# A one-core graph network layer: another order of the work within a step on TensorE, ScalarE and VectorE

## What is computed

```python
h = jnp.maximum(_layernorm(x, axis=-1), 0.0)
msg_input = jnp.concatenate([h[src], h[dst]], axis=1)
for t in range(4):
    m = jax.nn.relu(msg_input @ W1[t] + b1[t]) @ W2[t] + b2[t]
    msgs = msgs + jnp.where((edge_type == t)[:, None], m, 0)
agg = jax.ops.segment_sum(msgs, dst, num_segments=num_nodes)
gi = agg @ W_ih.T + b_ih          # i_r, i_z, i_n
gh = h @ W_hh.T + b_hh            # h_r, h_z, h_n
r = jax.nn.sigmoid(i_r + h_r)
z = jax.nn.sigmoid(i_z + h_z)
n = jnp.tanh(i_n + r * h_n)
out = x + (1.0 - z) * n + z * h
```

## Time and profile before

| | us |
|---|---|
| median of 3 runs | 1842.27 |
| lowest, highest | 1839.33, 1843.18 |
| profiled execution, its own time | 1840.2 |
| its span in the trace | 1838.3 |
| TensorE busy in the span | 1667.1 |
| VectorE, ScalarE, GpSimd busy | 1595.2, 1494.6, 1178.9 |

### The profile page before, as it was taken

The page is one execution under the profiler, slowest core; times in us unless marked ns, Lnnn a source line. Parts: engine busy times, 40 slices in busy tenths (PEclk is TensorE's granted clock), DMA queues, the critical chain, the costliest instruction groups (busy, mean ns, idle before and its releaser), DMA issues.

```text
span 1838.3 us, 43100 instructions
## 1 busy us (share of the span) xinstructions
PE 1667.1 (91%) x10182; PEld 1416.6 (77%) x10182; DVE 1595.2 (87%) x4186; ACT 1494.6 (81%) x3401; POOL 1178.9 (64%) x1982
## 2 busy tenths in 40 slices
PE   0226799999999999999999999999999999999998
PEld 0125688888888888888888888888888888888787
DVE  8597798989888988898889888989899989898776
ACT  0025789889888898898888888889898889888795
POOL 5777777776776777777765656666666566666310
PEclk9999899999999999999999999999999999999999
DMA  2225677777777776777677777777777777777653
GB/s 70 51 48 139 168 195 194 192 192 192 198 187 193 191 194 186 187 192 191 187 193 187 190 188 187 187 190 189 189 190 188 190 186 192 189 187 191 161 136 100
DMA packets 477071, 319.72 MB, mean 174 GB/s; under 512 B 106705, under 2 KB 463009, under 8 KB 476962
## 3 DMA queue, kind: packets, MB, share of 16 engines
q10 hardware_dynamic: 261792, 156.12, 28.6%
q1 hardware_dynamic: 185730, 106.99, 25.3%
q0 software_dynamic: 29440, 55.47, 11.8%
HBM read 211.65 MB, written 106.72 MB: 173 GB/s over the span
## 4 chain that ended last, share of the span: by engine, by line
PE 73%; ACT 8%; issue 4%; ACTq 3%; DVE 2%; DMA 0%; SPq 0%; POOL 0%; DVEq 0%; POOLq 0%
PE bank L1329 16%; PE bank L1331 12%; PE bank L1330 12%; PE bank L1409 10%; PE bank L1399 5%; PE bank L1391 5%; PE bank L1421 3%; PE bank L1420 3%; PE bank L1437 3%; ACT n_h L1194 3%; PE bank L1447 3%; ACT n_zc L1282 2%; ACTq L1211 2%; ACT e_r L1270 2%; ACTq L1232 2%
## 5 line engine op out<-in xcount | busy, mean ns | idle before, releaser
L580 POOL DMA_INDIRECT e_x<-in_x,rows_now x816 | 799.6, 980 | 241.7 <-issue 233.4
L1177 ACT ACTIVATE e_h<-e_x,shift,rstd 128x128 f32<-128x128 f32 x816 | 355.3, 493 | 93.6 <-DVE shift L1048 93.6
L1194 ACT ACTIVATE n_h<-n_x,shift,rstd 128x128 f32<-128x128 f32 x784 | 362.8, 489 | 2.1 <-issue 2.1
L1329 PE MATMUL bank<-n_h_hi,whh_hi 128*128 128x512 f32 x588 | 263.0, 447 | 25.3 <-ACT n_zc L1282 18.3
L1113 DVE TENSOR_TENSOR n_d<-bank,n_n 128x512 f32<-128x512 f32 x196 | 135.5, 691 | 160.7 <-ACT n_n L1278 149.1
L1329 PE MATMUL bank<-n_a_hi,wih_hi 128*128 128x512 f32 x588 | 249.3, 424 | 0.9 <-DVE bank L1083 0.9
L1071 DVE TENSOR_SCALAR n_sel<-iota,n_rel 128x256 fp32r<-128x256 f32 x784 | 237.8, 365 | 8.6 <-POOL n_rel L631 7.2
L1409 PE MATMUL bank<-n_sel,n_win 128*128 128x256 f32 x1568 | 234.9, 292 | 8.6 <-DVE n_sel L1071 8.4
L1331 PE MATMUL bank<-n_h_hi,whh_lo 128*128 128x512 f32 x588 | 232.9, 396 | 0.0
L1330 PE MATMUL bank<-n_h_lo,whh_hi 128*128 128x512 f32 x588 | 232.7, 396 | 0.0
L1331 PE MATMUL bank<-n_a_hi,wih_lo 128*128 128x512 f32 x588 | 232.3, 395 | 0.0
(11 more groups left out here) (179 smaller groups left out, 3895.4 us busy)
## 6 DMA issues: line engine op xcount, KB each, us to landing
n_win<-messages SPq DMA_DIRECT2D x1568, 64.2 KB
messages<-e_msg ACTq DMA_DIRECT2D x204, 257.0 KB, 2.7
n_x<-in_x ACTq DMA_DIRECT2D x195, 256.0 KB
out<-n_out ACTq DMA_DIRECT2D x195, 256.0 KB
e_x<-in_x,rows_now POOLq DMA_INDIRECT x816
rows_now<-lists SPq DMA_DIRECT2D x204, 2.0 KB
lists<-picks,list_rows POOLq DMA_INDIRECT x72
w<-in_W SPq DMA_DIRECT2D x1, 512.0 KB, 4.5
```

The lines of the kernel that those rows point to most:

```text
L580: G.indirect_dma_start(e_x[:, s, 2 * end + t, :], None, x, bass.IndirectOffsetOnAxis(ap=rows_now[:, s, t, end:end + 1], axis=0)).then_inc( ...
L1177: last = A.activation(e_h[:, s % 2, k, :], e_x[:, s, k, :], ACT.Relu, scale=rstd[:, slot, col + k:col + k + 1], bias=shift[:, slot, col + ...
L1194: last = A.activation(n_h[:, s % 2, cols], n_x[:, s, cols], ACT.Relu, scale=rstd[:, slot, col + 4 + k:col + 5 + k], bias=shift[:, slot, co ...
L1329: T.matmul(o, w_hi, v_hi, start=start, stop=False, skip_group_check=onto)
```

## The change

Nothing is computed in another way; instructions of a step change their place on three engines. TensorE: all gate products and the sums stand in one stretch (r, hn, sums, z, in), then transposes of h, first edge layer, transposes of n_e, transposes of the edge unit, second edge layer. ScalarE: the high part of the messages moves from the end of a step to the start of the next; one n_h moves ahead of n_a_hi, the two transfers stand directly behind n_a_hi; z comes ahead of tanh; n_h_hi comes behind tanh, then e_r, then e_ht. VectorE: n_h_lo moves from behind n_xh to between n_d and n_e. A wait of n_h_hi changes with it (for gate in of the group before instead of gate z). The core of the diff:

```diff
@@ VectorE
                 ln_part(i, m, 3)
-                if within(g, NG):
-                    dve.wait_ge(n_hhi, g + 1)
-                    V.tensor_tensor(n_h_lo[:, s % 2, :], bank[BT[s % 2]][:], n_h_hi[:, s % 2, :].bitcast(F32),
-                                    ALU.subtract).then_inc(n_hlo, 1)
                 ln_part(i, m, 4)
...
                 ln_part(i, m, 6)
+                g, s = i - LAG + 1, (m - LAG + 1) % UNROLL
+                if within(g, NG):
+                    dve.wait_ge(n_hhi, g + 1)
+                    V.tensor_tensor(n_h_lo[:, s % 2, :], bank[BT[s % 2]][:], n_h_hi[:, s % 2, :].bitcast(F32),
+                                    ALU.subtract).then_inc(n_hlo, 1)
+                g, s = i - LAG, (m - LAG) % 2
@@ ScalarE
             def step(i, m):
+                q, s = i - 10, (m - 10) % UNROLL
+                if within(q, UNITS):
+                    act.wait_ge(e_messaged, q + 1)
+                    act.wait_ge(e_tagged, q + 1)
+                    A.activation(e_msg[:, s, :, 0:D], bank[BE1][:, message_part].rearrange("p (t d) -> p t d", t=2),
+                                 ACT.Copy).then_inc(e_high, 1)
                 normalise_edges(i, m, (0, 1, 2))
...
+                normalise_nodes(i, m, (0,))
+                if within(g, NG):
+                    act.wait_ge(n_summed, g + 1)
+                    A.activation(n_a_hi[:, s, :], bank[BA][:], ACT.Copy).then_inc(n_ahi, 1)
+                store_out(i, m)
+                load_x(i, m)
+                normalise_nodes(i, m, (1, 2))
...
                     act.wait_ge(n_turned, g + 1)
                     if due(g - 1):
-                        act.wait_ge(n_gate_z, g - 1)
+                        act.wait_ge(n_gate_in, g - 1)
                     A.activation(n_h_hi[:, s, :], bank[BT[s]][:], ACT.Copy).then_inc(n_hhi, 1)
@@ TensorE
+                g, s = i - LAG, (m - LAG) % 2
+                if within(g, NG):
+                    pe.wait_ge(n_red, g + 1)
+                    gate(BRZ, 1, s, "ha").then_inc(n_gate_z, 1)
+                    pe.wait_ge(n_ted, g + 1)
+                    gate(BIN, 2, s, "a", onto=True).then_inc(n_gate_in, 1)
```

More of the change, by code:

```diff
@@ L1244, in step @@
                 store_messages(i, m)
[L1245 to L1250, removed]
+                g, s = i - LAG + 1, (m - LAG + 1) % 2
+                normalise_nodes(i, m, (0,))
[7 more added lines that the diff above has]
+                if within(g, NG):
+                    act.wait_ge(n_gate_z, g + 1)
+                    if due(g - 1):
+                        act.wait_ge(n_eed, g - 1)
+                    A.activation(n_zc[:, s, :], bank[BRZ][:], ACT.Sigmoid, bias=bneg[:, 1:2],
+                                 scale=-1.0).then_inc(n_zed, 1)
+                normalise_nodes(i, m, (3,))
+                if within(g, NG):
+                    act.wait_ge(n_gate_in, g + 1)
+                    if due(g - 1):
+                        act.wait_ge(n_ded, g - 1)
+                    A.activation(n_n[:, s, :], bank[BIN][:], ACT.Tanh, bias=bih[:, 2:3]).then_inc(n_ned, 1)
                 g, s = i - LAG + 1, (m - LAG + 1) % 2
@@ L1271, in step @@
                     last.then_inc(e_relued, 1)
[L1272 to L1285, removed]
+                q, s = i - 8, (m - 8) % 2
                 if within(q, UNITS):
[L1287 to L1290, removed]
+                    act.wait_ge(e_turned, q + 1)
+                    if due(q - 1):
+                        act.wait_ge(e_hid, q - 1)
+                    A.activation(e_ht[:, s, :], bank[BE0][:], ACT.Copy).then_inc(e_evaced, 1)
             pipeline(nc, act, LAST, LOOP_END, step)
@@ L1384, in step @@
                     gate(BHN, 2, s, "h").then_inc(n_gate_hn, 1)
[L1385 to L1392, removed]
                 g, s = i - LAG + 1, (m - LAG + 1) % 2
                 if within(g, NG):
[L1395 to L1400, removed]
                     pe.wait_ge(n_seled, g + 1)
@@ L1411, in step @@
                     last.then_inc(n_summed, 1)
+                g, s = i - LAG, (m - LAG) % 2
+                if within(g, NG):
+                    pe.wait_ge(n_red, g + 1)
+                    gate(BRZ, 1, s, "ha").then_inc(n_gate_z, 1)
+                    pe.wait_ge(n_ted, g + 1)
+                    gate(BIN, 2, s, "a", onto=True).then_inc(n_gate_in, 1)
+                g, s = i - LAG + 1, (m - LAG + 1) % 2
+                if within(g, NG):
+                    pe.wait_ge(n_normed, g + 1)
+                    if due(g - 1):
+                        pe.wait_ge(n_ded, g - 1)
+                    for k in range(TILES):
+                        last = T.transpose(bank[BT[s]][:, k * P:(k + 1) * P], n_h[:, s, k * D:(k + 1) * D], ident[:])
+                    last.then_inc(n_turned, 1)
                 q, s = i - 9, (m - 9) % 2
@@ L1422, in step @@
                     last.then_inc(e_hid, 1)
-                g, s = i - LAG, (m - LAG) % 2
+                g, s = i - LAG - 1, (m - LAG - 1) % 2
                 if within(g, NG):
[L1425 to L1428, removed]
+                    pe.wait_ge(n_eed, g + 1)
+                    if within(g + 1, NG):
+                        pe.wait_ge(n_ted, g + 2)
+                    elif due(g):
+                        pe.wait_ge(n_outed, g)
+                    for k in range(TILES):
+                        last = T.transpose(bank[BHN][:, k * P:(k + 1) * P], n_e[:, s, k * P:(k + 1) * P], ident[:])
+                    last.then_inc(n_back, 1)
+                q, s = i - 8, (m - 8) % 2
+                if within(q, UNITS):
+                    pe.wait_ge(e_normed, q + 1)
+                    if due(q):
+                        pe.wait_ge(e_evaced, q)
+                    for k in range(4):
+                        last = T.transpose(bank[BE0][:, k * P:(k + 1) * P], e_h[:, s, k, :], ident[:])
+                    last.then_inc(e_turned, 1)
                 q, s = i - 9, (m - 9) % 2
@@ L1438, in step @@
                     last.then_inc(e_messaged, 1)
[L1439 to L1448, removed]
                 if isinstance(i, int) and i == CHECK_STEP:
```

## The result

| | before | after | forecast |
|---|---|---|---|
| median, us | 1842.19 (4 runs, 1839.33 to 1843.18) | 1953.77 (4 runs, 1951.72 to 1954.11) | 1953 |
| ratio, 95% interval | | 1.0606 [1.0588, 1.0624] | 1.060 |
| profiled execution, its span | 1840.2, 1838.3 | 1953.48, 1951.6 | |
| a step | 8.35 | 8.93 | 8.93 |

The changed kernel is 6% slower.

A forecast was written before the change was run, and what follows sets the result against it. No engine is plainly the bound; a chain closing in one step sets 8.35 us. The longer new chain, 8.93, adds 0.58 x 195 = 113 us to 1840, giving 1953 us; range 1889 to 2010.

The forecast's parts named there:

- A: Chain through gate r, hn, sums, ScalarE's row to the late e_r, then message products: 8.65 us a step.
- B: Chain from tanh through VectorE's row with h_lo to n_sel, then sums and back to tanh: 8.93 us a step.
- The 1.22: ScalarE, n_a_hi to the next n_h with both transfers' issue between: 1.22 us, called uncertain, ends 0.49 and 1.45.
- the check of TensorE's arrival: TensorE reaches the sums before n_sel ends, so the sums wait 0.27 us, 0.16 of latency included.
- Rival 2: ScalarE's transfer issue hides while n_a_hi waits, so n_a_hi to n_h is 0.49: 1811 us, chance 0.05.
- VectorE's row, 4.67 from tanh to the end of n_sel: VectorE: tanh, n_d, h_lo, n_e, n_out, e_msg's low part and n_sel sum to 4.67 us.
- Rival 1: n_sel comes in time, so only the chain through e_r and the message products binds: 1899 us, chance 0.15.
- Rivals 3 and 4: TensorE packs its 7.92 with no wait, 1756 us, chance 0.03; or its clock falls, 2290 us, chance 0.02.
- rival 4: TensorE's granted clock drops to 1.2 GHz with 1.0 idle per step: +2.3 a step, 2290 us, chance 0.02.
- What would show it: Trace signs: r sigmoids 8.93 apart, idle before sums 40 to 60 us, before bias row 140 us, longer n_d wait.
- Joins of product kinds: TensorE: two fewer joins between product kinds gain at best 0.16 a step, 31 us; taken as 0.

The follow-up runs named there:

- e3: Changed kernel with e_msg's low part moved behind n_sel and n_xh moved ahead of the edge statistics on VectorE; 1889.85 us.
- e1: Changed kernel with VectorE's n_xh moved directly behind n_sel, ahead of the edge statistics and n_t; 1934.99 us.
- e2: Changed kernel with VectorE's low part of e_msg moved behind n_sel; 1951.67 us.
- e6: Changed kernel with ScalarE's issues of the out store and the x load both moved behind e_ht; 1940.36 us.
- e9: Changed kernel with ScalarE's out store issued behind n_zc and the x load behind tanh; 1860.05 us.
- e4: Changed kernel with ScalarE's e_r moved ahead of n_h_hi; 2028.58 us.
- e5: Changed kernel with TensorE's order of before, ScalarE and VectorE as changed; 2473.78 us.
- e7: Kernel before the change, with the out store issued behind n_h_hi and the x load behind n_zc; 1783.76 us.

## Why the prediction was right, and where its reasons were not

| chain | forecast | measured, with the others shortened |
|---|---|---|
| A: e_r, messages | 8.65 | 8.60 at most (e3) |
| B: h_lo, n_sel, sums | 8.93 | 8.84 (e1) |
| C: n_xh, load's issue | absent | 8.92 (e2) |
| the changed kernel | 8.93 | 8.93 |

*The number* (1953, 8.93 a step) was met within 1 us, but partly by luck. B was 0.09 shorter than its sum, and a chain that I hadn't walked was 0.08 longer than B is.

B's 0.09 comes mostly from two terms. The 1.22 was 1.16 without C's wait, and tanh to the start of the sums, 4.67 and 0.09 by the sum, was 4.71 on average (4.62 in the step shown). Between n_sel's end and the sums the sum has 0.09 and the check of TensorE's arrival 0.16; the rows show 0.05 (1011.18 to 1011.23).

*The step that failed* is in the part on ScalarE: I priced the two transfers by the time their issue takes, and said of the queues only that they keep their order. I did not ask what the load's issue waits for. It waits for n_xh of the same step, whose place on VectorE moved later against n_a_hi: before, n_xh was over by about 1011.7 (h_lo, behind it, starts at 1011.62 in the earlier trace rows) and the load was issued at 1011.94, so the wait was there and met: in most steps of the kernel before the load follows the store at that 0.18, wherever n_xh ends. Now n_xh ends at 1013.1, and the issue, which by the spacing of before (0.18) would have come at 1013.19, comes at 1013.38. That my 1.22 is close to the measured 1.25 comes of this: without the wait for n_xh it is 1.16 (e1). The same omission returned in e2 and e3, with the messages' store and its wait for the low part.

*n_a_hi to n_h, 1.22*: right in kind. The distance is 0.50 without the issue (e6, e9) and 1.16 with it; the sequencer did not issue while n_a_hi waited. In the changed kernel n_a_hi waited 0.42, and the store's issue began 0.14 after n_a_hi's start, not in the wait. Rival 2 is refuted with it. The Trainium skill (Perfetto Trace Analysis, DVE / Act Engine Instruction) has the sequencer free while an instruction waits; in none of these rows did ScalarE's use it.

*VectorE's row, 4.67 from tanh to the end of n_sel*: 4.57 in the step shown (1006.61 to 1011.18). Right within 0.1, and e4 (9.31 for 9.32) shows it as the row that binds when h_hi comes later.

*Rival 1 (only A, 1899)*: not the case; something near it is left when B and C are cut (e3, 1890).

*Rivals 3 and 4*: TensorE didn't pack, and the clock stayed at 1.00. But e5 shows that rival 4 can happen to another order of this kernel, at 2.7 idle in one piece, and that its price there is 0.65 a step on average and 1.7 in the steps that it hits (12.64 against 10.93), not 2.3.

*What would show it*: idle ahead of the bias row ended by e_r 114 us at the weight loads (forecast 140); ahead of the sums ended by n_sel 102 us there, though only 22.5 at the products themselves (forecast 40 to 60); in the rows of the step, n_a_hi waits 0.42 (0.55), e_msg 0.43 (0.6), n_d 1.65 (1.6). All have the right place and sign; some are smaller.

*Joins of product kinds, booked at 0*: nothing here speaks against it, but no run measured them alone. A's and B's sums are too long by 0.05 or more and by 0.09 in all.

**Where the 112 us are.** Two moved transfers take back 94 (e9). Yet the kernel before gains 54 by the same idea (e7), so with the issue out of the way in both, the new order is still 76 us behind (1860 against 1784, 0.39 a step). By the rows, VectorE's row is longer by h_lo behind tanh, and the transposes no longer cover n_sel; that this makes the 76 is argued, not shown. Putting h_lo back where it was, with the rest changed, wasn't tried.

## What to carry to other kernels

Here each transfer issued from ScalarE's queue took 0.38 to 0.6 us of its sequencer in the rows read, and that was hidden where it stood alone under an instruction of 0.6 to 0.7 (e7, e9). So give each transfer a long instruction of its own, and look at what its buffer waits for, since all that stands behind it in the queue inherits that wait (n_xh in chain C, the low part in e2 and e3). In a loop of several engines, walk every chain that closes in one step, those through a transfer's buffer too; where two are nearly equal, an edit that cuts one shows nothing until the other is cut. An order of one engine is good or bad only with the orders of the others (e5, e6).

## What the runs showed of the hardware that I had not expected

- **The clock after a long gap.** In e5, with TensorE idle 2.7 in one piece in each step, the granted clock fell from the 2.4 GHz level to 1.2 for stretches (0.54 from 1017 to 1020, 0.93 on average over 400 to 1700), and cost 0.65 a step. In the changed kernel, whose gaps are 0.6 at most in the step shown, it stayed at 1.00. The two steps of e5 shown hold the same work (x51) behind the same wait (2.74 ahead of the bias row at 1005.11, 2.73 at 1016.03), and one was slow.
- **A transfer's issue is nearly free in the right place.** n_zc to the next n_h is 0.61 with the store's issue between them (e9), 0.58 without it (1014.64 to 1015.22 in the changed kernel); behind n_a_hi both issues cost 0.66 (1.16 less 0.50).
